# One replicated denominator operand per chunk instead of one per head

## The chip, the cores and the metric

The kernel runs on all 8 cores of one Trainium2 chip, each core on its own part of the tokens and with no exchange between cores. The metric is the device time of the slowest core, in microseconds (us). In the names of the profile PE is TensorE, DVE is VectorE, ACT is ScalarE, POOL is GpSimd and SP is SyncE.

## The reference

One transformer layer on x of shape (4, 4096, 1024): x + LN(attention(LN(x))), then x + LN(FFN(LN(x))). Attention is linear attention with 16 heads of width 64 and 64 features; the FFN is a block-diagonal "rail" expansion, a GELU and a product with a 1024 x 16384 matrix. What the change touches is the denominator of the attention:

```python
def step(carry, inp):
    kv_s, k_s = carry
    qc, kc, vc = inp
    kv_prod = jnp.einsum('bhtf,bhtd->bhtfd', kc, vc)
    kv_cum = jnp.cumsum(kv_prod, axis=2) + kv_s[:, :, None]
    k_cum = jnp.cumsum(kc, axis=2) + k_s[:, :, None]
    ctx = jnp.einsum('bhtf,bhtfd->bhtd', qc, kv_cum)
    den = jnp.maximum(jnp.einsum('bhtf,bhtf->bht', qc, k_cum), 1e-06)
    out_c = ctx / den[..., None]
    return ((kv_cum[:, :, -1], k_cum[:, :, -1]), out_c)
```

## The kernel before, in words

Two cores share a sequence of 4096 tokens. Each owns 2048 of them and goes over 2048 more ("carry") to get the state that stands ahead of its own; on the cores that own the first half this state is scaled by 0. Tokens lie on the free axis, in chunks of 256; channels lie on the partitions, in 8 blocks of 128.

Each chunk has two stages. Stage A (stageA_gen) normalises x, makes Q, K and V and the features of Q and K. Stage B (emit_stageB) does the attention of the chunk, head by head, then the output projection, the layer norm and the residual add L301 into x_sb. First come 8 carry chunks, stage A only, with the update of the state; then stage A of main chunk 0; then for each of 8 main chunks stage B, with stage A of the next chunk interleaved: ahead of each head, pump() lets the generator emit its next piece. There are 11 calls' worth of pieces, so the last heads of a chunk stand alone ("plain heads"), and all heads of the last chunk do. Last comes the FFN, in two halves of 1024 tokens, with its weights streamed in.

Nothing schedules the work: each engine runs its instructions in the order in which the Python code emits them. T_, V_ and A_ emit for TensorE, VectorE and ScalarE, and each such instruction raises its engine's semaphore (sem_pe, sem_dv, sem_ac). P.snap gives the count so far, and waits=[("dv", n)] makes an instruction wait until VectorE has raised its own to n. L83 is the line of this wait in the helper, so a wait for a semaphore of VectorE shows in the profile as "DVEq L83".

The state is held as S_f (fp32) and its bf16 image S_bf, which is columns 1856 to 2383 of the shared buffer railsM: 8 blocks of 66 columns, for heads 2b (partitions 0 to 63) and 2b+1 (partitions 64 to 127). Columns 0 to 63 of a block are the sum of k times v, column 64 is the sum of k. S_bf is refreshed once at the end of a chunk (L596); within a chunk only S_f moves.

One head hh (lo = 0 or 64, slot sl = hh % 2 in PSUM) runs so:

- VectorE, L509: column 64 of the head's block is copied 64 times side by side into denrep, a 64x64 operand (columns 1792 to 1855 of railsM). It waits for slot_dv[sl], the count of VectorE at the end of the head two before.
- TensorE, L516 and L523: scores of k against q, 256 and 128 columns, which wait for the same slot_dv[sl] and for the transposed k of the chunk.
- VectorE, L529: scores times the causal mask, into ab_bf (also in railsM).
- TensorE, eight matmuls L535 to L569 behind one wait for L529: context from the state and from the scores, denominator from the state (L549, whose stationary operand is denrep) and from the scores, and the state's increment.
- VectorE, L576: denominator, at least 1e-6; ScalarE, L580 and L583: its inverse through Ln and Exp; VectorE, L587: context times inverse; VectorE, L591: increment added to S_f. Then slot_dv[sl] is taken.

A piece of stage A, where one is pumped, stands ahead of L509 on VectorE and ahead of L516 on TensorE. Ahead of head 0 the piece is L381, a copy of x into bf16. SyncE and GpSimd issue no work in stage B.

Of the kernel before, what the change touches and what calls it, by code (L numbers as in the profile page):

```python
# [11 lines left out]
AP = bass.AP  # L12
# [81 lines left out]
def build_nc(debug=(), n_carry=NCH, n_main=NCH, do_ffn=True, dumps=()):  # L94
# [33 lines left out]
    with es:  # L128
        sb = lambda n, shp, dt: es.enter_context(nc.sbuf_tensor(n, list(shp), dt))
        x_sb = sb("x_sb", (128, DB * NOWN), F32)  # L130
        railsM = sb("railsM", (128, 32 * 128), BF16)
# [19 lines left out]
        P = Prog(list(sems))  # L151

        def T_(fn, waits=()):
            P.emit("tensor", fn, waits, "pe")

        def V_(fn, waits=()):
            P.emit("vector", fn, waits, "dv")
# [26 lines left out]
        for db in range(DB):  # L184
# [17 lines left out]
           waits=[("dv", d_sv)])  # L202
# [7 lines left out]
           waits=[("dv", d_sv2)])  # L210
# [4 lines left out]
           waits=[("ac", P.snap("ac"))])  # L215
# [26 lines left out]
        ab_bf = railsM[:, 3424:3808]  # L242
        S_f = sba("S_f", (128, 8 * 66), F32)
        S_bf = railsM[:, 1856:2384]
        denrep = railsM[:, 1792:1856]
        dinv = railsM[:, 1536:1792]
        f32sB = sba("f32sB", (128, 1024), F32)
        mrB = sba("mrB", (128, 512), BF16)
# [244 lines left out]
        def emit_stageB(ci, parity, pump):  # L493
            qfb, kfb, kTb, vab = qf2[parity], kf2[parity], kT2[parity], va2[parity]
            kfT_done = marks[ci]["kfT_done"]
            slot_dv = [P.snap("dv")] * 2
            for hh in range(H):
                pump()
                sl = hh % 2
                base = sl * 1024  # L500
                bb, lo = hh // 2, (hh % 2) * 64
                kwo = {} if sl == 0 else {"tile_position": (0, 64)}
                kws = {} if sl == 0 else {"tile_position": (64, 64)}
                kwa = {} if sl == 0 else {"tile_position": (64, 0)}
                ctx0 = base + 512
                den0 = base + 768
                dS0 = base + 384

                V_((lambda v, hh=hh, sl=sl, lo=lo: v.tensor_copy(  # L509
                    denrep[sl * 64:sl * 64 + 64, 0:64],  # L510
                    AP(railsM, lo * 4096 + 1856 + 66 * (hh // 2) + 64,
                       [[4096, 64], [0, 64]]))),
                   waits=[("dv", slot_dv[sl])])

                T_((lambda t, base=base, bb=bb, lo=lo, kwa=kwa, kfb=kfb, qfb=qfb:
                    t.matmul(  # L516
# [4 lines left out]
                   waits=[("dv", slot_dv[sl]), ("dv", kfT_done)])  # L521
# [23 lines left out]
                    psB[lo:lo + 64, ctx0 + 128:ctx0 + 256],  # L545
                    vab[:, 1056 + 66 * hh:1056 + 66 * hh + 64],
                    ab_bf[:, 256:384], start=False, stop=True, **kwo)))
                T_((lambda t, den0=den0, hh=hh, lo=lo, sl=sl, bb=bb, kws=kws,
                    qfb=qfb: t.matmul(  # L549
                        psB[lo:lo + 64, den0:den0 + 256],  # L550
                        denrep[sl * 64:sl * 64 + 64, 0:64],
                        qfb[lo:lo + 64, bb * 256:bb * 256 + 256],
                        start=True, stop=False, **kws)))
                T_((lambda t, den0=den0, lo=lo, kwo=kwo: t.matmul(
# [27 lines left out]
                   waits=[("dv", dd)])  # L582
# [17 lines left out]
            for ob in range(8):  # L600
                for db in range(DB):
# [5 lines left out]
                       waits=[("dv", scan_done)] if (ob == 0 and db == 0) else [])  # L607
            po = P.snap("pe")
            for ob in range(8):
# [4 lines left out]
                   waits=[("pe", po)] if ob == 0 else [])  # L614
# [338 lines left out]
```

How the kernel before makes its waits and increments, by code:

```python
            def body(engobj, ename, elist):  # L74
                deep = engobj is nc.vector or engobj is nc.scalar
                for idx, (waits, fn, inc, inc_n) in enumerate(elist):
                    for s, v in waits:
                        if v > 0:
                            engobj.wait_ge(prog.sems[s], v)
                    ins = fn(engobj)
                    if inc is not None and signal_for.get((ename, idx), False):
                        if deep:
                            engobj.drain(fusable=True).then_inc(
                                prog.sems[inc], inc_n)
                        else:
                            ins.then_inc(prog.sems[inc], inc_n)
```

## Time and profile before

| What | us |
|---|---|
| Median of 2 runs (lowest, highest) | 4408.71 (4405.87, 4411.55) |
| The profiled execution | 4407.01 |
| Its span, core 4 (the slowest) | 4405.5 |
| Span of its fastest core, core 0 | 4351.4 |
| First L509, core 4: stage B of chunk 0 begins | 814.3 |
| L690 clears railsM for the FFN, core 4 | 2357.4 |
| VectorE busy, 1894 instructions | 1084.3 |
| TensorE matmuls busy, 10368 instructions | 2250.1 |

The span runs from the first to the last instruction of a core. A timeline's first number is the start from there, the second the duration. A bracket behind an instruction tells how long its engine was idle before it, and what ended that: another engine's instruction, a semaphore wait (L83), or "issue", when the profile shows nothing that it waited for.

### The profile page before, as it was taken

Reading aid. Unit: us, or ns where it says so; the run is one execution under the profiler, and the core shown is the slowest. Engines: PE = TensorE matmul, PEld = TensorE weight load, DVE = VectorE, ACT = ScalarE, POOL = GpSimd, SP = SyncE. Lnnn points to the kernel's source line nnn. Section 1 sums busy time; section 2 is a strip of 40 time slices with the busy share of each in tenths; the row PEclk is TensorE's granted clock in tenths of the full one; section 3 lists DMA queues with packets and bytes.
Section 4 is the critical chain, followed back from the end, with each engine's and each line's share of the span. In section 5 each row is a group of like instructions: output and inputs, shape, how many; then the busy total and the mean of one; then the engine's idle time right before and its main releaser. Section 6 shows DMA issues by size and latency. Waiting matters only on the chain.

```text
span 4405.5 us, 30746 instructions; the slowest of 8 cores (4351.4 to 4405.5 us)
## 1 busy us (share of the span) xinstructions
PE 2250.1 (51%) x10368; PEld 1014.3 (23%) x10368; DVE 1084.3 (25%) x1894; ACT 774.1 (18%) x1065; POOL 51.4 (1%) x73
## 2 busy tenths in 40 slices
PE   1333434444444354444444566666665566666665
PEld 0222222222222222222222222222222222222222
DVE  0333333333333333333334200000003200000003
ACT  0211112211121212121210211111111211111111
POOL 1000000000000000000000000000000000000000
PEclk9666666666666666666655688888878688888887
DMA  7000000000000000000000222222223022222221
GB/s 161 5 10 5 5 10 0 0 1 1 1 0 1 0 1 0 0 1 1 1 1 6 39 39 38 38 39 38 38 38 67 10 38 38 39 38 39 38 39 38
DMA packets 55079, 99.57 MB, mean 23 GB/s; under 512 B 2368, under 2 KB 18880, under 8 KB 53824
## 3 DMA queue, kind: packets, MB, share of 16 engines
q0 software_dynamic: 44880, 80.82, 11.7%
q1 hardware_dynamic: 10048, 16.79, 1.2%
q8 instruction: 88, 1.44, 0.1%
q14 instruction: 63, 0.52, 0.0%
HBM read 170.03 MB, written 8.39 MB: 41 GB/s over the span
## 4 chain that ended last, share of the span: by engine, by line
PE 46%; DVE 23%; DMA 11%; ACT 10%; issue 7%; DVEq 2%; ACTq 0%; POOL 0%; SPq 0%; POOLq 0%
PE psB L804 23%; DMA wc<-wcT 8%; PE psA L396 5%; PE psA L767 3%; DVE oacc L822 3%; PE psA L429 3%; DVE qk_bf L406 2%; DVE railsM L529 2%; DMA xa_bf<-x_carry 2%; PE psB L602 2%; DVEq L83 1%; DVE f32s L319 1%; DVE pn_bf L346 1%; PE psA L272 1%; PE psA L339 1%
## 5 line engine op out<-in xcount | busy, mean ns | idle before, releaser
L804 PE MATMUL psB<-hsl,wc 128*128 128x512 bf16 x4096 | 1048.8, 402 | 557.9 <-DMA wc<-wcT 437.6
L804 PEld LDWEIGHTS psB<-hsl,wc 128*128 128x128 bf16 x4096 | 374.6, 101 | 1097.7 <-issue 771.7
L778 ACT ACTIVATE hsl<-psA 128x512 bf16<-128x512 f32 x512 | 305.7, 597 | 1347.7 <-PE psA L767 1345.4
L822 DVE TENSOR_TENSOR oacc<-oacc,psB 128x2048 f32<-128x2048 f32 x56 | 128.1, 2287 | 1440.7 <-PE psB L804 1440.7
L396 PE MATMUL psA<-ln_bf,wqkv_bf 128*128 128x256 bf16 x1536 | 248.9, 340 | 85.2 <-DVEq L83 85.2
L266 PE MATMUL psA<-xa_bf,allones_bf 128*128 128x256 bf16 x256 | 58.9, 409 | 377.3 <-DMA xa_bf<-x_carry 215.2
L767 PE MATMUL psA<-ln,railsM 32*128 32x512 bf16 x512 | 207.1, 407 | 22.7 <-DVEq L83 13.5
L396 PEld LDWEIGHTS psA<-ln_bf,wqkv_bf 128*128 128x128 bf16 x1536 | 182.8, 122 | 145.8 <-issue 90.8
L580 ACT ACTIVATE f32sB<-f32sB 64x256 f32<-64x256 f32 x128 | 53.0, 414 | 869.3 <-DVEq L83 869.3
L429 PE MATMUL psA<-wqkv_bf,ln_bf 128*128 128x512 bf16 x512 | 168.7, 503 | 34.2 <-DVEq L83 34.2
L339 PE MATMUL psA<-qk_bf,omega_bf 64*64 64x256 bf16 x384 | 50.9, 414 | 211.4 <-DVEq L83 211.4
L262 ACT ACTIVATE sq_bf<-xa_bf 128x2048 bf16<-128x2048 bf16 x32 | 61.1, 1909 | 552.6 <-DVEq L83 299.5
L535 PE MATMUL psB<-qf_a,railsM 64*64 64x256 bf16 x64 | 22.1, 345 | 259.5 <-DVEq L83 259.5
L535 PE MATMUL psB<-qf_b,railsM 64*64 64x256 bf16 x64 | 23.4, 366 | 245.1 <-DVEq L83 245.1
L406 DVE TENSOR_SCALAR qk_bf<-psA,bqkv_sb 128x256 bf16<-128x256 f32 x192 | 92.8, 483 | 202.0 <-PE psA L396 183.0
L314 PE MATMUL psA<-sq_bf,blockones_bf 128*128 128x256 bf16 x192 | 47.4, 398 | 152.8 <-ACTq L83 116.2
L266 PEld LDWEIGHTS psA<-xa_bf,allones_bf 128*128 128x128 bf16 x256 | 32.6, 136 | 396.9 <-issue 384.8
L576 DVE TENSOR_SCALAR f32sB<-psB 64x256 f32<-64x256 f32 x128 | 54.0, 422 | 241.9 <-PE psB L569 239.5
L767 PEld LDWEIGHTS psA<-ln,railsM 32*128 32x128 bf16 x512 | 46.7, 92 | 254.7 <-issue 254.7
L429 PEld LDWEIGHTS psA<-wqkv_bf,ln_bf 128*128 128x128 bf16 x512 | 60.4, 123 | 136.1 <-issue 113.1
L587 DVE TENSOR_TENSOR ctx_bf<-psB,railsM 64x256 bf16<-64x256 f32 x128 | 54.0, 422 | 151.7 <-ACTq L83 151.7
L319 DVE TENSOR_SCALAR f32s<-psA 128x1024 f32<-128x1024 f32 x48 | 58.8, 1225 | 113.5 <-PE psA L314 113.5
(150 smaller groups left out, 2064.0 us busy)
## 6 DMA issues: line engine op xcount, KB each, us to landing
wc<-wcT POOLq DMA_DIRECT2D x32, 2048.0 KB, 18.3
x_sb<-x_own SPq DMA_DIRECT2D x8, 1024.0 KB, 23.3
y_out<-oacc SPq DMA_DIRECT2D x8, 1024.0 KB, 4.4
wqkv_bf<-wqkvT POOLq DMA_DIRECT2D x8, 768.0 KB, 48.8
xa_bf<-x_carry POOLq DMA_DIRECT2D x8, 512.0 KB, 6.1
wout_bf<-woutT POOLq DMA_DIRECT2D x8, 256.0 KB, 67.8
rut_bf<-rut POOLq DMA_DIRECT2D x4, 128.0 KB, 6.1
omega_bf<-omega POOLq DMA_DIRECT2D x2, 128.0 KB, 16.0
```

What stands on the lines that cost most here:

```text
L266: T_((lambda t, db=db: t.matmul(ps[:, 0:256], allones_bf[:, :], xb[:, db * 256:(db + 1) * 256], start=(db == 0), stop=(db == DB - 1))), wa ...
L319: V_((lambda v: v.tensor_scalar(f32s[:, 0:1024], psA[:, 0:1024], 1e-24, None, op0=ALU.max)), waits=[("pe", p0)])
L339: t.matmul(psA[lo:lo + 64, bb4 * 256:(bb4 + 1) * 256], omega_bf[lo:lo + 64, hcur * 64:(hcur + 1) * 64], src_bf[lo:lo + 64, bb * 256:(bb + ...
L396: T_((lambda t, jj=jj, jb=jb, db=db: t.matmul(psA[:, jj * 256:(jj + 1) * 256], wqkv_bf[:, db * 3072 + jb * 128:db * 3072 + (jb + 1) * 128] ...
L406: v.tensor_scalar(dst[:, dstoff + jj * 256:dstoff + (jj + 1) * 256], psA[:, jj * 256:(jj + 1) * 256], bqkv_sb[:, jb0 + jj:jb0 + jj + 1], N ...
L429: T_((lambda t, sub=sub, db=db, oh=oh: t.matmul(psA[:, oh * 512:(oh + 1) * 512], ln1_bf[:, db * 256 + sub * 128:db * 256 + sub * 128 + 128 ...
L529: V_((lambda v, base=base: v.tensor_tensor(ab_bf[:, 0:384], psB[:, base:base + 384], mask384_bf[:, 0:384], op=ALU.mult)), waits=[("pe", pa)])
L602: T_((lambda t, ob=ob, db=db: t.matmul(psB[:, ob * 256:(ob + 1) * 256], wout_bf[:, db * 1024 + ob * 128:db * 1024 + (ob + 1) * 128], ctx_b ...
L767: zsl=zsl: t.matmul(psA[:, zsl * 512:(zsl + 1) * 512], railsM[rg * 32:(rg + 1) * 32, q4 * 128:(q4 + 1) * 128], ln3[pbase:pbase + 32, dbl * ...
L778: A_((lambda a, fcl=fcl, zsl=zsl, hb=hb: a.activation(hb[:, fcl * 512:(fcl + 1) * 512], psA[:, zsl * 512:(zsl + 1) * 512], AF.Gelu)), wait ...
L804: t.matmul(psB[:, ob * 512:(ob + 1) * 512], wcbufs[fcl // 8][:, (fcl % 8) * 1024 + obi * 128: (fcl % 8) * 1024 + (obi + 1) * 128], hb[:, f ...
L822: V_((lambda v, g=g, obg=obg: v.tensor_tensor(AP(oacc, obg * 4096 + g * 512, [[8 * 1024, 128], [1024, 4], [1, 512]]), AP(oacc, obg * 4096 ...
```

## The change

The per-head copy L509 is taken out. In its place one copy at the start of emit_stageB, ahead of head 0, replicates column 64 of all 8 blocks of S_bf, on all 128 partitions, into a new denrep of 512 columns (2384 to 2895 of railsM, free in this stage). It waits for all TensorE work emitted so far. slot_dv is taken behind it, so the first two heads' score matmuls wait for it too. The denominator matmul reads the 64 columns of its own block.

```diff
-        denrep = railsM[:, 1792:1856]
+        denrep = railsM[:, 2384:2896]
...
             kfT_done = marks[ci]["kfT_done"]
+            V_((lambda v: v.tensor_copy(
+                AP(railsM, 2384, [[4096, 128], [64, 8], [1, 64]]),
+                AP(railsM, 1856 + 64, [[4096, 128], [66, 8], [0, 64]]))),
+               waits=[("pe", P.snap("pe"))])
             slot_dv = [P.snap("dv")] * 2
...
-                V_((lambda v, hh=hh, sl=sl, lo=lo: v.tensor_copy(
-                    denrep[sl * 64:sl * 64 + 64, 0:64],
-                    AP(railsM, lo * 4096 + 1856 + 66 * (hh // 2) + 64,
-                       [[4096, 64], [0, 64]]))),
-                   waits=[("dv", slot_dv[sl])])
...
-                        denrep[sl * 64:sl * 64 + 64, 0:64],
+                        denrep[lo:lo + 64, bb * 64:bb * 64 + 64],
```

The order of the instructions on the other engines stays; on VectorE it changes at two kinds of places. VectorE before the change, at the start of main chunk 1 (L301 is the residual add of chunk 0, L278 to L285 the first steps of a layer norm of stage A):

```order
L301 TENSOR_TENSOR x_sb<-x_sb,ctx_bf 128x8x256
L381 CAST xa_bf<-x_sb 128x2048 [waits sem_din]
L509 COPY railsM<-railsM 64x64 [waits sem_dv]
L529 TENSOR_TENSOR railsM<-psB,railsM 128x384 [waits sem_pe]
L576 TENSOR_SCALAR f32sB<-psB 64x256 [waits sem_pe]
L587 TENSOR_TENSOR ctx_bf<-psB,railsM 64x256 [waits sem_ac]
L591 TENSOR_TENSOR S_f<-S_f,psB 64x65
L278 TENSOR_SCALAR f32s<-psA 128x256 [waits sem_pe]
L280 TENSOR_TENSOR f32s<-f32s 128x256
L282 SCALAR_TENSOR_TENSOR f32s<-psA,f32s 128x256
```

and VectorE at the same place after the change, where L496 is the new copy, and the lines from L527 on are those from L529 on of before, numbered two lower:

```order
L301 TENSOR_TENSOR x_sb<-x_sb,ctx_bf 128x8x256
L496 COPY railsM<-railsM 128x512 [waits sem_pe]
L381 CAST xa_bf<-x_sb 128x2048 [waits sem_din]
L527 TENSOR_TENSOR railsM<-psB,railsM 128x384 [waits sem_pe]
L574 TENSOR_SCALAR f32sB<-psB 64x256 [waits sem_pe]
L585 TENSOR_TENSOR ctx_bf<-psB,railsM 64x256 [waits sem_ac]
L589 TENSOR_TENSOR S_f<-S_f,psB 64x65
L278 TENSOR_SCALAR f32s<-psA 128x256 [waits sem_pe]
L280 TENSOR_TENSOR f32s<-f32s 128x256
L282 SCALAR_TENSOR_TENSOR f32s<-psA,f32s 128x256
```

The new copy stands between L301 and L381, with a wait for sem_pe, and the mask multiply follows L381 directly. VectorE in the last chunk's first two heads, before:

```order
L301 TENSOR_TENSOR x_sb<-x_sb,ctx_bf 128x8x256
L509 COPY railsM<-railsM 64x64 [waits sem_dv]
L529 TENSOR_TENSOR railsM<-psB,railsM 128x384 [waits sem_pe]
L576 TENSOR_SCALAR f32sB<-psB 64x256 [waits sem_pe]
L587 TENSOR_TENSOR ctx_bf<-psB,railsM 64x256 [waits sem_ac]
L591 TENSOR_TENSOR S_f<-S_f,psB 64x65
L509 COPY railsM<-railsM 64x64 [waits sem_dv]
L529 TENSOR_TENSOR railsM<-psB,railsM 128x384 [waits sem_pe]
```

and after:

```order
L301 TENSOR_TENSOR x_sb<-x_sb,ctx_bf 128x8x256
L496 COPY railsM<-railsM 128x512 [waits sem_pe]
L527 TENSOR_TENSOR railsM<-psB,railsM 128x384 [waits sem_pe]
L574 TENSOR_SCALAR f32sB<-psB 64x256 [waits sem_pe]
L585 TENSOR_TENSOR ctx_bf<-psB,railsM 64x256 [waits sem_ac]
L589 TENSOR_TENSOR S_f<-S_f,psB 64x65
L527 TENSOR_TENSOR railsM<-psB,railsM 128x384 [waits sem_pe]
```

From the second head on the mask multiply stands directly behind the add into S_f, where the copy stood between them; this is so in every head ahead of which no piece of stage A stands, and in the others it stands directly behind the piece.

## Rows read from the trace of the kernel before

**Rows 1.** The page's first line, all cores.

```profile
span 4405.5 us, 30746 instructions; the slowest of 8 cores (4351.4 to 4405.5 us)
```

**Rows 2.** The page's chain that ended last, shares of the span by engine.

```profile
PE 46%; DVE 23%; DMA 11%; ACT 10%; issue 7%; DVEq 2%; ACTq 0%; POOL 0%; SPq 0%; POOLq 0%
```

**Rows 3.** Who waited, core 4: engine, tile, line <- releaser: us, times, longest.

```profile
PE psB L535 <- DVEq L83: 504.5, 128, 9.1
```

**Rows 4.** VectorE's groups: line, operation, tiles, count | busy us, mean ns | idle before.

```profile
L529 DVE TENSOR_TENSOR railsM<-psB,railsM 128x384 bf16<-128x384 f32 x128 | 71.4, 558 | 25.4 <-issue 24.9 <-PE psB L523 0.5
...
L319 DVE TENSOR_SCALAR f32s<-psA 128x1024 f32<-128x1024 f32 x48 | 58.8, 1225 | 113.5 <-PE psA L314 113.5
...
L576 DVE TENSOR_SCALAR f32sB<-psB 64x256 f32<-64x256 f32 x128 | 54.0, 422 | 241.9 <-PE psB L569 239.5 <-PE psA L396 2.4
...
L509 DVE COPY railsM<-railsM 64x64 bf16<-64x64 bf16 x128 | 24.2, 189 | 26.4 <-DVEq L83 26.4
...
L328 DVE TENSOR_SCALAR xa_bf<-xa_bf 128x1024 bf16<-128x1024 bf16 x48 | 20.5, 426 | 118.4 <-ACTq L83 118.4
...
L596 DVE CAST railsM<-S_f 128x528 bf16<-128x528 f32 x8 | 3.5, 435 | 0.9
```

**Rows 5.** Timeline of one plain head: start, duration, engine, line [idle before <-releaser].

```profile
1981.79 0.21 DVE L591 TENSOR_TENSOR S_f<-S_f,psB 64x65 f32<-64x65 f32 x1
1982.19 0.19 DVE L509 COPY railsM<-railsM 64x64 bf16<-64x64 bf16 x1 [0.19 <-DVEq L83]
1982.57 0.56 DVE L529 TENSOR_TENSOR railsM<-psB,railsM 128x384 bf16<-128x384 f32 x1 [0.19 <-issue]
...
1983.31 0.39 PE L535 MATMUL psB<-qf_b,railsM 64*64 64x256 bf16 x1 [3.32 <-DVEq L83]
...
1985.18 0.43 DVE L576 TENSOR_SCALAR f32sB<-psB 64x256 f32<-64x256 f32 x1 [2.05 <-PE psB L569]
1985.19 0.31 PE L523 MATMUL psB<-qf_b,kf_b 64*128 64x128 bf16 x1
...
1988.11 0.56 DVE L529 TENSOR_TENSOR railsM<-psB,railsM 128x384 bf16<-128x384 f32 x1 [0.19 <-issue]
```

**Rows 6.** Timeline, VectorE, a copy behind L591.

```profile
1161.23 0.23 DVE L591 TENSOR_TENSOR S_f<-S_f,psB 64x65 f32<-64x65 f32 x1
1161.64 1.23 DVE L460 COPY kT_a<-psT 128x2048 bf16<-128x2048 bf16 x1 [0.19 <-issue]
```

**Rows 7.** Timeline, first heads of main chunk 1 and of the last chunk.

```profile
1223.09 1.23 DVE L381 CAST xa_bf<-x_sb 128x2048 bf16<-128x2048 f32 x1 [0.19 <-issue]
...
1223.36 0.31 PE L523 MATMUL psB<-qf_a,kf_a 64*128 64x128 bf16 x1
...
2240.56 0.19 DVE L509 COPY railsM<-railsM 64x64 bf16<-64x64 bf16 x1 [0.19 <-DVEq L83]
...
2241.24 0.56 DVE L529 TENSOR_TENSOR railsM<-psB,railsM 128x384 bf16<-128x384 f32 x1 [0.49 <-PE psB L523]
```

**Rows 8.** Stretches from L301 to L301: length, busy by engine, granted clock, DMA, GB/s.

```profile
1013.22:1220.61 207.39, 92.67 (x484) 52.81 (x484) 71.58 (x138) 39.20 (x52) 0.00 (x0) 0.62 0.00 0
...
1627.02:1828.98 201.96, 87.11 (x484) 50.75 (x484) 71.58 (x138) 39.20 (x52) 0.00 (x0) 0.63 0.00 0
...
2033.75:2238.08 204.33, 88.82 (x484) 51.44 (x484) 71.58 (x139) 39.20 (x52) 0.00 (x0) 0.63 0.00 1
2238.08:2354.02 115.94, 47.33 (x240) 25.39 (x240) 39.59 (x96) 15.99 (x35) 0.00 (x0) 0.56 0.00 0
```

**Rows 9.** Timeline, V's projection at both clocks; L576 behind a head at the high clock.

```profile
1954.53 5.60 PE L429 MATMUL psA<-wqkv_bf,ln_bf 128*128 128x512 bf16 x16
...
1964.34 3.63 PE L429 MATMUL psA<-wqkv_bf,ln_bf 128*128 128x512 bf16 x16
...
1057.29 0.43 DVE L576 TENSOR_SCALAR f32sB<-psB 64x256 f32<-64x256 f32 x1 [1.41 <-PE psB L569]
```

**Rows 10.** Who waited, core 4, in the FFN.

```profile
PE psB L804 <- DMA wc<-wcT: 437.6, 14, 33.2
```

More of the change, by code:

```diff
@@ L547, in emit_stageB @@
                     ab_bf[:, 256:384], start=False, stop=True, **kwo)))
-                T_((lambda t, den0=den0, hh=hh, lo=lo, sl=sl, bb=bb, kws=kws,
+                T_((lambda t, den0=den0, hh=hh, lo=lo, bb=bb, kws=kws,
                     qfb=qfb: t.matmul(
                         psB[lo:lo + 64, den0:den0 + 256],
-                        denrep[sl * 64:sl * 64 + 64, 0:64],
+                        denrep[lo:lo + 64, bb * 64:bb * 64 + 64],
                         qfb[lo:lo + 64, bb * 256:bb * 256 + 256],
```

## The prediction

> **What bounds the kernel now.** I read the cores first: they end between 4351.4 and 4405.5 us [rows 1]; the last is core 4, and every number below is its own. The profiled execution took 4407.0 us for a span of 4405.5, so 1.5 us lie outside the span; the median of the runs shown is 4408.7, 1.7 above it, and I add nothing for that. The chain that ended last names no single engine: TensorE 46%, VectorE 23%, DMA 11%, ScalarE 10% [rows 2]. That is the picture of stages that take turns. The change touches one of them, the part of attention that I call stage B. There the question is whether VectorE's small copy L509 is in the chain or beside it; its 0.55% share of the span says nothing of that.
>
> Two readings settle it. First, who waits in stage B: TensorE stands before L535 in all 128 heads, 504.5 us in total, for VectorE [rows 3]. L535 is released by the mask multiply L529. So TensorE is the one that waits, and whatever stands ahead of L529 on VectorE delays it. Second, what ended the wait of L529 itself: 24.9 of its 25.4 us of idle time are "issue", and 0.5 us are TensorE's L523, in one head only [rows 4]. So the two score matmuls L516 and L523, which write what L529 reads, are finished in 127 of 128 heads before VectorE gets there. One plain head shows it: S_f's add L591 ends at 1982.00, the copy runs 1982.19 to 1982.38, the mask starts at 1982.57, and TensorE, idle for 3.32 us, starts L535 at 1983.31; the next head's L523 runs from 1985.19 to 1985.50, while that head's mask comes only at 1988.11, 2.6 us later [rows 5]. The copy and the gap that belongs to it are in series with everything in a head. That holds in heads with a piece of stage A too, since the piece's VectorE work comes before the copy and its TensorE work before L516.
>
> **What goes.** In each of 127 heads the stretch from the end of L591 (or of a piece of stage A) to the start of L529 is gap, copy, gap. By group: 24.2 us of copies and 26.4 us of idle time before them, over 128: 0.189 + 0.206 = 0.395 us a head [rows 4]. The 0.19 before L529 stays, if the mask standing directly behind L591 starts as soon after it as after a copy. Rows show this: L460, a copy that waits for a TensorE semaphore long raised, as L529 will, stands directly behind L591 and starts 0.19 us after its end [rows 6]. So 127 x 0.395 = 50.2 us go. In the 128th, head 0 of the last chunk, the copy is hidden: VectorE had 0.49 us more to wait for L523 anyway [rows 7]. It gives nothing. L549, which reads the replicated column, reads as many columns and partitions as before and stays as it is.
>
> **What comes.** Eight copies of 128x512, one a chunk, behind L301 and ahead of head 0. The trace has no such copy. Nearest by shape is L509 itself with its repeated element: 64 columns in 0.189 us. Nearest by size is L596, 528 columns in 0.435 us, fp32 to bf16 [rows 4]. From the two, (0.435 - 0.189) / 464 = 0.53 ns a column: 512 columns are 0.43 us, which I take. Below it cannot be faster than L509's 0.19; above, at the rate of operations that read PSUM, (1.225 - 0.558) / (1024 - 384) = 1.04 ns a column from L319 and L529, it takes 0.558 + 128 x 1.04 ns = 0.69 us. With a gap of 0.19 that is 0.62 us a chunk, 5.0 us in all (3.0 to 7.1).
>
> L328, a bf16 operation, moves 1024 columns in 0.426 us [rows 4], which would suggest 0.29 us for 512. The Trainium skill says why this does not carry over (Vector Engine (DVE) Microarchitecture Reference, section 5.1): pairing two 16-bit values in a read wants an innermost step of 1, and a one-source copy that repeats an element takes the mode that splits the work over two ports instead, two results a cycle. By that rule the copy costs 0.43 us; by L328's it would cost 0.29, a difference of 1 us over eight.
>
> Is all of it on the path? slot_dv is now taken behind the copy, so L516 and L523 of head 0 wait for it, and they start 0.62 us later. In seven chunks L381 (1.23 us) follows the copy on VectorE, covers both matmuls, which were done at 1223.67, 0.65 us before it was [rows 7], so that their own delay costs nothing. The copy itself is in VectorE's queue and delays L381 and the mask by its whole 0.62 us. In the last chunk there is no L381: L516, L523 and then the mask follow the copy in series, again 0.62 us. So 8 x 0.62 in full. Its TensorE semaphore is no wait: all TensorE work emitted before it is the layer norm whose sums L278 has consumed, or in chunk 0 the transposes behind L460. Nothing is queued behind it that a DMA needs; SyncE and GpSimd have no work in stage B.
>
> **The sum.** 50.2 - 5.0 = 45.2 us, all before the FFN, which starts that much earlier on all eight cores together. 4407.0 - 45.2 = **4361.8 us**, 1.0% less. I write 4362.
>
> **What the clock and the FFN add to the range.** TensorE's granted clock in stage B is a mixture of 1.2 and 2.4 GHz: 0.62 to 0.63 of full in chunks with stage A, 0.56 in the last [rows 8]. The same instructions took 207.39 us in one chunk and 201.96 in another; the mean of six is (2238.08 - 1013.22) / 6 = 204.14 [rows 8]. Shorter heads shift where the clock rises and falls. If all seven chunks fell like the best one, 7 x 2.2 = 15 us more would go; all like the worst, 7 x 3.3 = 23 us would come back. In the FFN TensorE waits 437.6 us for weights [rows 10] and the cores differ by 54 us at the end [rows 1], though their order hardly changes when all shift alike; I allow 5 us. With the copy's ends (2 us either way) the likeliest case runs from 4362 - 22 = 4340 to 4362 + 30 = 4392.
>
> **Rivals.**
>
> *Only the copy's own time goes.* If the 0.206 us ahead of the copy is the tail of L591 (its drain and signal) and the mask would have to sit through it besides its own, each head gives 0.189: 127 x 0.189 - 5.0 = 19 us, so 4388. For it: the gap before L509 is of the same size as other gaps. Against: [rows 6]. Chance 7%.
>
> *The clock rises with the denser heads.* A head at the low clock waits 2.05 us for L569, one at the high clock 1.41, and 239.5 us over 127 waits is a mean of 1.89, so about a quarter of the heads run at the high clock: (2.05 - 1.89) / 0.64 [rows 4, 5, 9]. If the other 95 turned, 95 x 0.64 = 61 us more would go, and pieces like V's projection would fall from 5.60 to 3.63 us [rows 9]; of the 56 pieces of that size in seven chunks I take a quarter as cold now, 14 x 1.97 = 28 us more. 4362 - 61 - 28 = 4273, past the 2% that about marks what a measurement here can tell from no change. For it: L535's idle stretch falls from 3.32 to 2.94 us. The Trainium skill (TensorE: Matmul & The Clock Gate, What's actually happening) has the clock throttled by default and released by activity, which points this way. Against: the last chunk, whose heads are all plain, holds 0.56 [rows 8] though TensorE's long idle stretch is 3.3 of each 5.54 us there, and 0.4 of 5.54 us is a small change. Chance 6%; a partial form of it is in the lower part of the range.
>
> *The clock falls out of step (slower).* The dense pieces of stage A and the output projection are worth most of the high-clock time. Going cold costs 5.60 - 3.63 = 1.97 us for 16 x 512 columns [rows 9]. A chunk has 4 x 32 x 256 + 2 x 16 x 512 + 64 x 256 = 65,536 columns of such work, eight times that: at most 15.8 us a chunk, 110 us in seven. All cold would give 4362 + 110 = 4472, slower than before. It decides against the change from a loss of 45.2 / 7 = 6.5 us a chunk, some three of eight such pieces. Against it: the worst chunk so far lies 3.3 above the mean, and TensorE becomes busier, not idler. Chance 4%.
>
> *Forecast*: 83%.
>
> **Chances.** Forecast 83 (all within 2%, which is 88 us), copy's time only 7 (within 2%), clock up 6 (faster by over 2% in 5 of them), clock down 4 (mostly within 2%, over it in 2). Faster by over 2%: 0.05; within: 0.93; slower: 0.02. The range is the likeliest case's own, 4340 to 4392, which takes in the copy-only case at 4388 and leaves out the two cases of the clock, one in ten.
>
> **What would show each step.** Right: no copy between L591 and the mask, 0.19 us between them, plain heads 0.38 to 0.40 us shorter (5.54 to 5.14); eight copies of about 0.43 us; six middle chunks with a mean near 198.4 us (204.14 - 16 x 0.395 + 0.62); TensorE's wait before L535 down by about 50 us; the FFN from 2354 on unchanged in length within some 10 us. Wrong: the mask waiting on L523 in many heads, a gap of 0.4 us behind L591, a copy over 0.7 us, a granted clock in stage B that differs by more than 0.02, or an FFN that grows by as much as stage B loses.

## The result and the profile after

The ratio of the changed kernel to the one before is 0.9899, 95% interval 0.9871 to 0.9927: about 45 us less, between 32 and 57. The median of 15 runs is 4368.4 us, that of 14 runs of the kernel before 4413.2; the ratio leaves out the runs in which the cores of one die were granted a lower clock than the others. The forecast was 4362 us, 1.0% less, with 93% on a change within 2%. The profiled execution of the changed kernel took 4352.8 us, its slowest core is core 3.

VectorE's groups of the changed kernel, core 3, with the columns of [rows 4]:

```profile
L527 DVE TENSOR_TENSOR railsM<-psB,railsM 128x384 bf16<-128x384 f32 x128 | 71.3, 557 | 25.5 <-issue 24.6 <-PE psB L521 0.9
L574 DVE TENSOR_SCALAR f32sB<-psB 64x256 f32<-64x256 f32 x128 | 54.0, 422 | 242.9 <-PE psB L567 242.9
L496 DVE COPY railsM<-railsM 128x512 bf16<-128x512 bf16 x8 | 3.4, 427 | 1.5 <-issue 1.5
```

The new copy takes 0.427 us, eight times, with a gap of 0.19 (1.5 / 8) and no wait for TensorE. The mask L527 still waits for nothing but the hand-over from the instruction ahead of it (0.19 us), save one head with 0.9 us. TensorE's wait ahead of the first matmul behind the mask fell from 504.5 us [rows 3] to this, in the view of who waited:

```profile
PE psB L533 <- DVEq L83: 459.3, 128, 8.7
```

That is 45.2 us less, on the engine that waits, where about 50 were forecast (the two profiles' slowest cores are compared; core for core it is 43 to 46). Most of what is missing is in the seven heads behind the 16 transposes L454 on TensorE. On core 4 these took 1.8 to 1.9 us in all seven chunks before, at the low clock, and some 1.1 us in five of the seven after, at the high one; TensorE was ready earlier there and waited longer. The timeline of the last chunk's first heads, the same place as the lower rows of [rows 7]:

```profile
2205.03 2.29 DVE L301 TENSOR_TENSOR x_sb<-x_sb,ctx_bf 128x2048 f32<-128x2048 f32 x1
2207.51 0.43 DVE L496 COPY railsM<-railsM 128x512 bf16<-128x512 bf16 x1 [0.19 <-issue]
2208.80 0.56 DVE L527 TENSOR_TENSOR railsM<-psB,railsM 128x384 bf16<-128x384 f32 x1 [0.86 <-PE psB L521]
...
2213.54 0.22 DVE L589 TENSOR_TENSOR S_f<-S_f,psB 64x65 f32<-64x65 f32 x1
2213.94 0.56 DVE L527 TENSOR_TENSOR railsM<-psB,railsM 128x384 bf16<-128x384 f32 x1 [0.19 <-issue]
...
2218.69 0.23 DVE L589 TENSOR_TENSOR S_f<-S_f,psB 64x65 f32<-64x65 f32 x1
2219.10 0.56 DVE L527 TENSOR_TENSOR railsM<-psB,railsM 128x384 bf16<-128x384 f32 x1 [0.19 <-issue]
```

Two things are to be seen. Between L589 and the mask 0.18 to 0.19 us are left, and a plain head takes 5.16 us (2213.94 to 2219.10) where it took 5.54. And in head 0 the mask starts 3.77 us behind L301's start, where it started 3.16 behind it (2241.24 against 2238.08 [rows 7, 8]): the copy with its gap, 0.61 us, is in the chain there, and nothing is gained.

**Where the time went, stage by stage.** From the first instruction of stage B of chunk 0 (L516 before, the new copy after) to the last start of L301, the mean over the eight cores is 1539.9 us before and 1502.0 after, 37.9 less, where 45.2 were forecast. VectorE works or waits through all of it, so its time can be split without a rest. In us from the start of the first mask on, mean over eight cores; "own" is its work (537.0 before, 515.9 after) with the gaps that no other engine ended (96.7 and 72.4):

| Kernel | VectorE's own | waits for TensorE | waits for ScalarE | together |
|---|---|---|---|---|
| before | 633.7 | 602.7 | 301.7 | 1538.2 |
| after | 588.3 | 609.9 | 301.8 | 1500.0 |

VectorE's own time fell by 45.4 us, which is what the prediction's sum gave. The 7 us that are missing are in its waits for TensorE, and TensorE's instructions are the same. What changed is the clock that they were granted. In that stretch V's projections L429 kept TensorE busy for 73.2 us where it was 67.6 (mean of the six cores whose profile has all their records), the output projection 72.6 for 69.0, the projections of Q and K 145.5 for 149.9, and the transposes 9.1 for 12.9. These last 3.8 us give VectorE nothing, since it does not wait for the transposes. VectorE's wait for one of V's two buffers, core 4 before and core 3 after:

```profile
L443 DVE CAST va_b<-psA 128x1024 bf16<-128x1024 f32 x8 | 9.8, 1224 | 22.0 <-PE psA L437 22.0
L443 DVE CAST va_b<-psA 128x1024 bf16<-128x1024 f32 x8 | 9.8, 1225 | 27.5 <-PE psA L437 27.5
```

A plain head became 0.38 us shorter and not 0.395. Most gaps ahead of L509 are 0.187 us; the mean of 0.206 holds seven longer ones, as this in VectorE's timeline of the kernel before:

```profile
2302.57 0.19 DVE L509 COPY railsM<-railsM 64x64 bf16<-64x64 bf16 x1 [0.54 <-DVEq L83]
```

Such gaps are not the copy's. VectorE has 11 of them in stage B before, ahead of L509, L529 and L610, and 5 after, at the same instructions on all eight cores, and they follow each other at distances near multiples of 48 of its instructions. But with six fewer of them another 2.1 us went, so that the mean was a fair price after all: 127 x 0.38 + 2.1 - 5.0 = 45.4. Without them the sum is 43.3 us. The chunks, L301 to L301, with the columns of [rows 8] (core 3):

```profile
1010.32:1204.94 194.62, 84.69 (x484) 49.26 (x484) 68.99 (x123) 39.20 (x52) 0.00 (x0) 0.64 0.00 0
1204.94:1404.64 199.70, 88.96 (x484) 51.03 (x484) 68.98 (x123) 39.20 (x52) 0.00 (x0) 0.62 0.00 0
1404.64:1605.97 201.33, 92.21 (x484) 52.39 (x484) 68.97 (x123) 39.20 (x52) 0.00 (x0) 0.60 0.00 0
...
2205.03:2316.47 111.44, 48.48 (x240) 25.83 (x240) 36.98 (x81) 16.00 (x35) 0.00 (x0) 0.55 0.00 0
2316.47:4351.30 2034.83, 1300.01 (x4992) 468.57 (x4992) 295.93 (x322) 354.72 (x564) 31.33 (x37) 0.79 0.21 38
```

The same 484 matmuls keep TensorE busy for 84.69 us in one chunk and for 92.21 in another, VectorE's 68.98 and ScalarE's 39.20 us stay, and the chunk is 6.7 us longer: what varies is the clock that TensorE is granted. The last row is the FFN, 2034.8 us on the slowest core, against 2051.5 on the slowest before (2354.05 to 4405.50); over all cores the mean is 2016.8 against 2025.7. The FFN's share of the difference between the two profiled executions is no effect of the change, as the repeats below show.

### The profile page after: what moved, and what is told of

It is laid out like the page before. It is cut to its first block, busy times and chain, and to the rows that moved or that the text cites. A ratio compares the mean times of both kernels' runs of the same rounds, so it can differ in the third digit from the quotient of the medians.

```text
span 4351.3 us, 30386 instructions; the slowest of 8 cores (4319.0 to 4351.3 us)
## 1 busy us (share of the span) xinstructions
PE 2271.1 (52%) x10368; PEld 1014.9 (23%) x10368; DVE 1063.5 (24%) x1774; ACT 774.2 (18%) x1065; POOL 51.4 (1%) x73
## 4 chain that ended last, share of the span: by engine, by line
PE 47%; DVE 23%; DMA 11%; ACT 10%; issue 7%; DVEq 2%; ACTq 0%; POOL 0%; SPq 0%; POOLq 0%
PE psB L802 24%; DMA wc<-wcT 8%; PE psA L396 5%; PE psA L765 3%; DVE oacc L820 3%; PE psA L429 3%; DVE qk_bf L406 2%; PE psB L600 2%; DVE railsM L527 2%; DMA xa_bf<-x_carry 2%; DVE pn_bf L346 1%; DVE f32s L319 1%; PE psA L272 1%; DVEq L83 1%; PE psA L339 1%
## 5 line engine op out<-in xcount | busy, mean ns | idle before, releaser
L802 PE MATMUL psB<-hsl,wc 128*128 128x512 bf16 x4096 | 1062.2, 406 | 525.7 <-DMA wc<-wcT 405.4
L429 PE MATMUL psA<-wqkv_bf,ln_bf 128*128 128x512 bf16 x512 | 177.9, 524 | 33.5 <-DVEq L83 33.5
L339 PE MATMUL psA<-qk_bf,omega_bf 64*64 64x256 bf16 x384 | 50.9, 413 | 211.4 <-DVEq L83 211.4
L406 DVE TENSOR_SCALAR qk_bf<-psA,bqkv_sb 128x256 bf16<-128x256 f32 x192 | 92.8, 483 | 196.3 <-PE psA L396 177.3
L429 PEld LDWEIGHTS psA<-wqkv_bf,ln_bf 128*128 128x128 bf16 x512 | 62.5, 127 | 142.5 <-issue 124.6
L323 ACT ACTIVATE f32s<-f32s 128x1024 f32<-128x1024 f32 x48 | 50.7, 1056 | 203.1 <-DVEq L83 203.1
(150 smaller groups left out, 2051.5 us busy)
## 6 DMA issues: line engine op xcount, KB each, us to landing
wqkv_bf<-wqkvT POOLq DMA_DIRECT2D x8, 768.0 KB, 48.6
```

The costliest lines, as they stand in the source:

```text
L339: t.matmul(psA[lo:lo + 64, bb4 * 256:(bb4 + 1) * 256], omega_bf[lo:lo + 64, hcur * 64:(hcur + 1) * 64], src_bf[lo:lo + 64, bb * 256:(bb + ...
L406: v.tensor_scalar(dst[:, dstoff + jj * 256:dstoff + (jj + 1) * 256], psA[:, jj * 256:(jj + 1) * 256], bqkv_sb[:, jb0 + jj:jb0 + jj + 1], N ...
L429: T_((lambda t, sub=sub, db=db, oh=oh: t.matmul(psA[:, oh * 512:(oh + 1) * 512], ln1_bf[:, db * 256 + sub * 128:db * 256 + sub * 128 + 128 ...
L802: t.matmul(psB[:, ob * 512:(ob + 1) * 512], wcbufs[fcl // 8][:, (fcl % 8) * 1024 + obi * 128: (fcl % 8) * 1024 + (obi + 1) * 128], hb[:, f ...
```

## The experiments

"Stage B" in this section is the stretch just named, from its first instruction to the last start of L301, mean over eight cores. "By the rows" is what the instructions on VectorE account for against 1539.9 us before: 0.38 us for a small copy that leaves the chain of a head, 0.62 us for a chunk's copy. These sums leave out the longer gaps, whose number changes from kernel to kernel (11 before, 5 after) and with it up to 2.4 us; the table behind the last profiles has them in.

### One copy more per head

```diff
+                # the same L509 again, directly behind itself
+                V_(... v.tensor_copy(denrep[sl * 64:sl * 64 + 64, 0:64], ...),
+                   waits=[("dv", slot_dv[sl])])
```

> The kernel before with L509 issued twice in each head. Theory (each such copy is in the chain of 127 heads): every head grows by 0.395 us, plain heads from 5.54 to 5.93 us, the whole by 50 us, ratio 1.011. Rival (VectorE has slack, the copy is mostly hidden and the change's gain came from the clock or the FFN): under 15 us, ratio below 1.004. On the clock: if the length of a chunk depends on where the clock's changes fall, the six middle chunks will not all be 6.3 us longer but scatter by some 5 us around that.

Measured: ratio 1.0138, interval 1.0052 to 1.0223. VectorE's groups of this kernel:

```profile
L509 DVE COPY railsM<-railsM 64x64 bf16<-64x64 bf16 x128 | 24.2, 189 | 24.8 <-DVEq L83 24.8
L514 DVE COPY railsM<-railsM 64x64 bf16<-64x64 bf16 x128 | 24.2, 189 | 24.8 <-DVEq L83 24.8
```

A second copy costs 0.189 + 0.194 us in every head, 48.6 us in 127 heads, as the theory says; the rival with a hidden copy falls, since the interval excludes it. Stage B is 1598.7 us, 58.8 more, so 10 us come on top: VectorE's waits for TensorE are 612.5 us for 602.7. The six chunks did not scatter here: on all cores all are between 211.4 and 211.8 us. That part of the expectation was wrong.

### The same copies behind the mask

```diff
-                V_(... tensor_copy(denrep ...), waits=[("dv", slot_dv[sl])])
...
                 da = P.snap("dv")
+                V_(... tensor_copy(denrep ...))
+                dc = P.snap("dv")
...
-                        start=True, stop=False, **kws)))
+                        start=True, stop=False, **kws)), waits=[("dv", dc)])
```

> The kernel before with all 128 small copies kept, but each issued behind its head's mask multiply, and L549 waiting for it. Theory (it is the place on VectorE and not the work): the copy runs while VectorE would wait 2.05 us for TensorE, it ends 0.3 to 0.4 us behind the mask, L549 comes 0.9 us or more behind it and does not wait; heads as short as after the change (5.15 us), 50 us less than before, ratio about 0.9885, with VectorE's busy time unchanged at 1084 us. Rival (the 20 us less of VectorE's work is what counts, or the shorter program): no more than 10 us gained.

Measured: ratio 0.9888, interval 0.983 to 0.9947, stage B 1492.5 us, where the rows give 1539.9 - 48.3 = 1491.6. The timeline of a plain head:

```profile
2239.74 0.56 DVE L523 TENSOR_TENSOR railsM<-psB,railsM 128x384 bf16<-128x384 f32 x1 [0.19 <-issue]
2240.41 0.19 DVE L527 COPY railsM<-railsM 64x64 bf16<-64x64 bf16 x1
2240.47 0.39 PE L535 MATMUL psB<-qf_b,railsM 64*64 64x256 bf16 x1 [2.97 <-DVEq L83]
...
2241.25 0.42 PE L549 MATMUL psB<-qf_b,railsM 64*64 64x256 bf16 x1
2241.60 0.42 PE L554 MATMUL psB<-railsM,allones_bf 128*64 128x256 bf16 x1
...
2242.34 0.42 DVE L576 TENSOR_SCALAR f32sB<-psB 64x256 f32<-64x256 f32 x1 [1.75 <-PE psB L569]
...
2244.88 0.56 DVE L523 TENSOR_TENSOR railsM<-psB,railsM 128x384 bf16<-128x384 f32 x1 [0.19 <-issue]
```

The copy ends at 2240.60, L549 starts at 2241.25 in its turn, and the copy only takes 0.3 us out of VectorE's wait for L569 (1.75 for 2.05). The head is 5.14 us long. All 128 copies are still there (VectorE's busy time is 1084.9 us), and the time is that of the changed kernel: what the change gained was their place ahead of the mask, not their work. This is shown, and the rival of less work falls. (The copies have no wait for a semaphore here; the next experiment has the price of that, 0.07 us each.)

### The small copy without its wait

```diff
-                   waits=[("dv", slot_dv[sl])])
+                   )
```

> The kernel before, with the small copy L509 left in its place but without its wait for VectorE's own semaphore. Theory (the copy and a gap of 0.206 us that belongs to its wait are in series with the head): the idle time ahead of the copy falls from 0.206 to about 0.12 us, the gap that L591 has behind L587 without a wait; 0.09 us a head, 11 us in all, ratio to before about 0.9975, and plain heads of 5.45 us for 5.54. Rival (the gap is the tail of L591, its drain and signal, and no wait's doing): the gap stays at 0.2 us and the time stays.

Measured: ratio 0.9988, interval 0.9952 to 1.0025, which cannot tell 0.9975 from 1. The group can:

```profile
L509 DVE COPY railsM<-railsM 64x64 bf16<-64x64 bf16 x128 | 24.2, 189 | 15.4 <-issue 0.4
```

The mean gap fell from 26.4 / 128 = 0.206 to 0.120 us, the usual one from 0.187 to 0.118. So 0.07 us of each gap were the wait for VectorE's own semaphore, which had long been raised, and 0.12 belong to one more instruction in the queue; the other 0.017 of the mean are longer gaps, of which seven stood ahead of the copy before and one here. The theory holds for the gap: 9 us for the waits, 10 with the longer gaps. VectorE's own time fell by 9.5 us. Stage B is 1535.7 us, only 4.2 less: 5.4 us came back in VectorE's waits for TensorE.

### The chunk's copy where VectorE waits for the output projection

```diff
-            V_(chunk copy, waits=[("pe", P.snap("pe"))])
+            if ci == 0:
+                V_(chunk copy, waits=[("pe", P.snap("pe"))])
...
             V_((lambda v: v.tensor_copy(S_bf[:, :], S_f[:, :])))
             scan_done = P.snap("dv")
+            if ci + 1 < n_main:
+                V_(chunk copy, waits=[("pe", pc)])
```

> The changed kernel with the chunk's copy for chunks 1 to 7 issued directly behind the refresh of S_bf (L594) of the chunk before, where VectorE waits 9 us for the output projection. Theory: 7 x 0.62 = 4.3 us less than after the change, ratio to before about 0.9889 against 0.9899; the last chunk's mask of head 0 starts 3.16 us behind L301's start instead of 3.77. Rival (the copy at the chunk's start is hidden already beside TensorE's first scores): the same start of the mask and no gain. The total cannot tell these apart within its interval, the timeline can.

Measured: ratio 0.9913, interval 0.9878 to 0.9949, no better than the change itself. Core 0's timeline, the last chunk:

```profile
2189.43 0.43 DVE L595 CAST railsM<-S_f 128x528 bf16<-128x528 f32 x1
2190.05 0.43 DVE L598 COPY railsM<-railsM 128x512 bf16<-128x512 bf16 x1 [0.19 <-issue]
...
2213.31 2.29 DVE L301 TENSOR_TENSOR x_sb<-x_sb,ctx_bf 128x2048 f32<-128x2048 f32 x1
2216.47 0.56 DVE L528 TENSOR_TENSOR railsM<-psB,railsM 128x384 bf16<-128x384 f32 x1 [0.86 <-PE psB L522]
```

The mask starts 3.16 us behind L301 again, as forecast, so the 0.61 us a chunk did leave the chain. Yet stage B is 1503.6 us, 11 above what the rows give (1539.9 - 43.3 - 4.3 = 1492.3): the 4 us were won and lost again. VectorE's waits for TensorE, which should be 4 us shorter with the copy in them, are 611.6 us for 609.9, and V's projections took 78.0 us for 73.2.

### The changed kernel again, and with a shift in time

> The changed kernel itself, once more, for its chunk lengths alone (from L301 to L301). If these are set by the program and the point at which the clock's changes fall in it, they should lie between 194 and 203 us again with a mean of 198 to 200 over six chunks and eight cores, but need not have the same order as in the first profile.

> The changed kernel with one extra write of a scratch buffer on VectorE at the start of stage B of chunk 0 only, some 1.1 us, so that all that follows is later against the clock's changes and else the same. Theory (what a chunk gives back or gains through TensorE's clock depends on when the clock changes fall in it, and not on the shorter heads as such): the chunks' lengths take other values than in the other runs of the changed kernel, in the same band of 194 to 203 us, and their mean stays within 1.5 us. Rival (the give-back of 0.7 us a chunk is a property of heads of 5.15 us): the same mean to 0.2 us and the same list.

```diff
             slot_dv = [P.snap("dv")] * 2
+            if ci == 0:
+                V_(lambda v: v.memset(f32sB[:, 0:1024], 0.0))
```

Measured: 4372.4 us for the repeat and 4364.5 for the shift, one execution each. The repeat's chunks have a mean of 198.5 us (the first profile's 198.9), and its first two are 196.3 and 198.0 on all eight cores, as on five cores of the first profile. The shift (the write took 0.91 us) gives other ones, core 0:

```profile
1006.52:1206.98 200.46, 90.14 (x483) 51.64 (x484) 68.97 (x123) 39.20 (x52) 0.00 (x0) 0.64 0.00 0
1206.98:1405.65 198.67, 88.00 (x483) 50.71 (x484) 68.99 (x123) 39.20 (x52) 0.00 (x0) 0.63 0.00 0
1405.65:1600.26 194.61, 84.38 (x483) 49.26 (x484) 68.99 (x123) 39.20 (x52) 0.00 (x0) 0.64 0.00 0
```

with a mean of 198.7 over all. Core 0 had 196.33, 198.00 and 199.65 us there in the first profile, so single chunks move by up to 5 us when the program is 1 us later. They can do so without a shift too: core 4 had 200.62 and 202.01 us in its first two chunks in the first profile and 196.33 and 198.00 in the repeat. The mean moves by less than 0.5 either way, so these two runs don't tell a shift's mean from a repeat's. Stage B is 1498.9 us in the repeat and 1500.6 in the shifted kernel (1501.7 less the write and its gap, which lie in it there), against 1502.0; the slowest core's FFN was 2053.0 and 2048.3 us, against 2034.8 in the first profile and 2051.5 before. The 17 us by which the first profile's FFN was shorter on the slowest core were luck of that execution.

Where the clock takes time is best seen in a piece with no other engine in it, the 64 matmuls of the output projection. Timelines of the first profile of the changed kernel, core 3:

```profile
1379.76 10.02 PE L600 MATMUL psB<-ctx_bf,wout_bf 128*128 128x256 bf16 x64 [3.23 <-DVEq L83]
...
1781.78 8.72 PE L600 MATMUL psB<-ctx_bf,wout_bf 128*128 128x256 bf16 x64 [3.25 <-DVEq L83]
```

Both start after the same idle time and the same heads. The stretches of the two, with the granted clock behind the engines' columns:

```profile
1379.76:1389.78 10.02, 10.02 (x64) 7.51 (x64) 0.00 (x0) 0.00 (x0) 0.00 (x0) 0.70 0.01 2
1781.78:1790.50 8.72, 8.72 (x64) 6.91 (x64) 0.00 (x0) 0.00 (x0) 0.00 (x0) 0.81 0.00 0
```

A mean of 0.70 of 2.4 GHz against 0.81: the granted clock rose from 1.2 to 2.4 GHz at 1385.68 in the one, 5.9 us behind its start, and at 1785.04 in the other, 3.3 behind it.

### The kernel before again, and with the same shift

The rows give 1496.6 us for stage B of the changed kernel, and its profiles show more. Either the first profile of the kernel before was a lucky draw of the clock, or the clock answers to the change.

> The kernel before, once more, for its chunks. Theory (its first profile was a favourable draw of the clock): the mean of the six middle chunks rises from 203.9 us to 204.3 or more, and stage B from 1539.9 us to 1542 to 1550, so that the changed kernels fall into line with what the rows give. Rival (it is no draw: the clock answers in its own way to the length of a head): again 203.9 within 0.3, and stage B again within 2 us of 1539.9. The plain head is 5.54 us by both, and the time 4400 to 4425 us.

> The kernel before with one write of about 0.9 us ahead of the first head, the shift given to the changed kernel before. Theory (a favourable draw): other single chunks, and with them a mean of the six middle chunks at 204.3 us or more and stage B at 1542 to 1550 us. Rival: single chunks move, the mean stays at 203.9 within 0.3 us and stage B within 3 us of 1540.

```diff
             slot_dv = [P.snap("dv")] * 2
+            if ci == 0:
+                V_(lambda v: v.memset(f32sB[:, 0:1024], 0.0))
```

Measured, in the profiled executions: 4457.7 us (4514.8 in another one) and 4398.9. The first time can't be compared, since it is made in the FFN: cores 0 and 1 took 2095.6 and 2093.1 us for it at a granted clock of 0.76, the others 2001 to 2055 at 0.80. In stage B two other cores stand apart, 2 and 3, which were granted 0.58 to 0.59 in chunk 0 and the first three middle chunks where 0.62 to 0.63 stand on the rest. With them the mean of the chunks is 204.3 us and stage B 1543.4; the six other cores have 203.9 and 1539.6. Core 0's first two chunks in that profile, where it had 204.27 and 201.86 before:

```profile
1023.15:1227.44 204.29, 89.36 (x483) 51.88 (x484) 71.59 (x139) 39.20 (x52) 0.00 (x0) 0.63 0.00 0
1227.44:1429.29 201.85, 86.66 (x483) 50.63 (x484) 71.59 (x138) 39.20 (x52) 0.00 (x0) 0.63 0.00 0
```

And core 0 with the shift:

```profile
1014.44:1219.20 204.76, 89.72 (x483) 51.89 (x484) 71.61 (x139) 39.20 (x52) 0.00 (x0) 0.62 0.00 0
1219.20:1420.10 200.90, 86.01 (x483) 50.18 (x484) 71.58 (x139) 39.20 (x52) 0.00 (x0) 0.64 0.00 0
```

With the shift the mean is 202.7 us and stage B 1535.1, less the write and its gap. So the theory of a lucky draw falls: in the repeat four of the six cores drew chunks of the first profile again, and another moment gives less time, not more. The rival is right for the repeat and wrong for the shift, whose mean moved by 1.3 us (202.4 to 203.0 on its cores, 203.1 to 204.2 on those without the shift); it is one profile. Like for like, stage B is 39 us shorter by the change without the shift (1539.8 against 1500.5, the means of two profiles each) and 35 with it (1535.1 against 1500.6). The split of VectorE's time, as in the result's table (the repeat of the kernel before without cores 2 and 3):

| Kernel | VectorE's own | waits for TensorE | waits for ScalarE | together |
|---|---|---|---|---|
| before | 633.7 | 602.7 | 301.7 | 1538.2 |
| before, again | 633.9 | 602.2 | 301.7 | 1537.9 |
| before, shifted | 632.9 | 599.6 | 300.9 | 1533.3 |
| changed | 588.3 | 609.9 | 301.8 | 1500.0 |
| changed, again | 588.5 | 606.5 | 301.8 | 1496.8 |
| changed, shifted | 588.3 | 608.9 | 301.1 | 1498.4 |
| one copy more per head | 682.8 | 612.5 | 301.3 | 1596.6 |
| small copy without its wait | 624.2 | 608.1 | 301.6 | 1534.0 |
| small copies behind the mask | 624.2 | 565.3 | 301.6 | 1491.1 |
| chunk's copy late | 588.3 | 611.6 | 301.7 | 1501.5 |

VectorE's own time is the same in every profile of one kernel to 0.2 us. By the change it falls by 45.4 us without the shift and by 44.6 with it. TensorE gave back 6 us without the shift and 9 with it.

### The masks one head ahead

The experiments say that any instruction of VectorE between a head's context multiply and the next mask is in series with TensorE. The mask itself, and the way through ScalarE, need not be. In this version the scores of head h+1 are issued directly behind the matmuls of head h, its mask between the maximum and the context multiply of head h, and the next piece of stage A behind head h's work instead of ahead of head h+1's scores. Head 0's piece, scores and mask come ahead of the loop:

```diff
-                pump()
...
+                if hh + 1 < H:
+                    pa = scores(hh + 1)      # the two score matmuls
                 V_(... f32sB ... 1e-6, op0=ALU.max ...), waits=[("pe", pc)])
                 dd = P.snap("dv")
+                if hh + 1 < H:
+                    da = mask(hh + 1, pa)    # the mask multiply
                 A_(... AF.Ln ...)
                 A_(... AF.Exp ...)
                 V_(... ctx_bf ...)
                 V_(... S_f ...)
                 slot_dv[sl] = P.snap("dv")
+                if hh + 1 < H:
+                    pump()
```

> The changed kernel with each head's mask multiply moved further forward on VectorE: the mask of head h+1 is issued right behind the maximum of head h (L574 there), where VectorE waits 1.18 us for ScalarE, and the scores of head h+1 directly behind head h's matmuls, with the next piece of stage A behind them. Theory (what VectorE does between a head's context multiply and the next mask is in series with TensorE, and so is the way through ScalarE): a plain head is then mask 0.56, matmuls 2.05, maximum 0.42 and a gap of 0.19, 3.2 us instead of 5.15; 15 x 1.9 = 29 us in the last chunk, and about 30 us in each of seven pumped chunks (5 plain heads of 1.9, ten heads with a piece of 2 or so), together 240 us, to about 4130, ratio to before 0.936 (range 0.92 to 0.96). Rival (the chain is bound elsewhere, by pieces of stage A through ScalarE and VectorE): only the plain heads gain, 29 + 7 x 9.5 = 95 us, ratio 0.968.

> The run with the masks ahead, and the chunk's copy behind the refresh of S_bf as well. Theory: 4 us less than that run, at most; within the intervals no difference. It is run as the version that could be the fastest, on the same chip as the other.

Measured: ratio 0.9297 (0.9255 to 0.9339) and 0.9285 (0.9238 to 0.9332), medians 4109.5 and 4100.0 us. The two cannot be told apart. VectorE's timeline of the first, a plain head:

```profile
1965.03 0.42 DVE L586 TENSOR_SCALAR f32sB<-psB 64x256 f32<-64x256 f32 x1 [0.84 <-PE psB L577]
1965.63 0.56 DVE L523 TENSOR_TENSOR railsM<-psB,railsM 128x384 bf16<-128x384 f32 x1 [0.19 <-issue]
1966.63 0.42 DVE L599 TENSOR_TENSOR ctx_bf<-psB,railsM 64x256 bf16<-64x256 f32 x1 [0.44 <-ACTq L83]
1967.16 0.21 DVE L603 TENSOR_TENSOR S_f<-S_f,psB 64x65 f32<-64x65 f32 x1
1968.24 0.43 DVE L586 TENSOR_SCALAR f32sB<-psB 64x256 f32<-64x256 f32 x1 [0.86 <-PE psB L577]
1968.86 0.56 DVE L523 TENSOR_TENSOR railsM<-psB,railsM 128x384 bf16<-128x384 f32 x1 [0.19 <-issue]
```

The head is 3.23 us long, the 3.2 of the expectation, and the mask now fills VectorE's wait for ScalarE (0.44 us left of 1.18). TensorE's wait ahead of the first matmul behind the mask:

```profile
PE psB L543 <- DVEq L83: 104.5, 79, 2.7
```

It was 459.3 us in 128 heads. The last chunk fell from 111.4 to 81.8 us, 29.6 where 29 were expected, and the middle chunks from 198.9 to 161.2 on average, 37.8 where 30 were expected. Five plain heads make 1.93 x 5 = 9.7 of that; the other 28 come from eleven heads with a piece of stage A, 2.6 us each. The rival, in which only plain heads gain, falls. The granted clock of these chunks rose too, to a mean of 0.67 from 0.63. Three things moved at once here (scores, mask, pieces), and no run parts them.

## Why the prediction was right, point by point

- **The copy is in the chain, in 127 of 128 heads.** Right, and shown from both sides: one more copy a head makes the kernel longer by about as much as the change made it shorter, and the same copies behind the mask cost nothing.
- **0.395 us a head, 50.2 us.** Right, with a little luck. A plain head became 0.38 us shorter, and 127 x 0.38 are 48.3. The mean gap that the prediction took also held seven longer gaps that belong to no copy; six fewer of these in the changed kernel gave the other 2 us. Between L589 and the mask stand 0.18 to 0.19 us. The rival "only the copy's own time goes" (4388 us) falls by that gap. It was in the range, and the total's interval reaches close to it (0.9927 is 4381 us); the rows decide it, not the total.
- **Eight copies of 0.43 us and 0.19 us of gap, all on the path, 5.0 us.** Right: 0.427 and 0.19, and the mask of the last chunk's head 0 came 0.61 us later. Two results a cycle for a repeated element (the Trainium skill, Vector Engine (DVE) Microarchitecture Reference, section 5.1) had given the prediction an estimate of 0.43 us, and the trace agrees with its 0.427.
- **45.2 us in all, TensorE's wait down by about 50.** VectorE's own time fell by 45.4 us, stage B by 37.9; the ratio gives 45 with 12 either way. That the total came out so near the forecast is in part luck, since stage B gave 7 us less. TensorE's wait fell by 45.2 us and not by 50, the most of that behind the transposes that ran at the high clock.
- **The clock's edge of 15 us gained to 23 us lost.** The size was right and the middle was not: the prediction took it as even. Against the first profile of before, VectorE's waits for TensorE were 7, 4 and 6 us longer in the three profiles of the changed kernel (its repeat and the shift among them), 5 without the wait and 10 with two copies; with the late copy 13 us came back and with the copies behind the mask 2 to 3. That the profile of before was a lucky draw was tried and fell. So a small part of what VectorE gives up comes back as TensorE's time at the lower clock, 6 to 9 us of 45 for this change, like for like. In the total this hardly shows, since the FFN of single executions varies by more.
- **The FFN unchanged within some 10 us.** The first profile missed this by 7 us (17 shorter); with three profiles of the changed kernel, at 2034.8, 2053.0 and 2048.3 us on the slowest core against 2051.5, no effect of the change is seen, and single profiles of one program differ by 18 us there, more than the 10 us of that line.
- **The rivals of the clock.** Neither came in the size that was named. The granted clock of middle chunks stayed at a mean of 0.63. What did come is a small form of the second: at the same mean clock the high stretches fell in other places, V's projections and the output projection took 9 us more, those of Q and K 4 less, and the transposes 4 less, for which VectorE does not wait. The rise did come, to 0.67, when a head fell to 3.2 us.

What stays open: how the clock's part follows from the length of a head. It is no simple rule of "shorter heads, slower clock", since the kernel with two copies, with longer heads, lost too, and the one with the copies behind the mask lost only 2 to 3 us with a head of 5.14 us. It depends on the moment, and perhaps differently in the two kernels (a shift of 0.91 us moved the mean chunk by 1.3 us in one and by less than 0.5 in the other, one profile each). No run varied the length of a head finely enough.

## What to carry to other kernels

An instruction's share of the span does not tell its price. Ask instead what ended the wait of the instruction behind it: here the mask waited for nothing but its place in VectorE's queue, and each copy of 0.19 us ahead of it cost 0.38 with its gap, 127 times. If what an operand needs is known early, issue it where the engine waits in any case. And when one small instruction turns out to be in the chain, look at all that share its place: moving scores, mask and pieces, so that the mask fills the wait for ScalarE, was worth six times the copy.

## What the hardware showed that was not expected

A wait for a semaphore that is long raised is not free: 0.07 us on VectorE (the usual gap 0.187 with it, 0.118 without), about a third of such a small copy. VectorE has longer gaps of some 0.5 us that belong to no instruction but to its place: 11 in stage B before, the same on all eight cores and in the repeat, at distances near multiples of 48 of its instructions, and 8 in other places when one write was added ahead. The same 64 matmuls behind the same idle time took 8.72 or 10.02 us, by when TensorE's clock rose from 1.2 to 2.4 GHz, and in this program, whose stages repeat with one period, these draws are not independent. The kernel before drew the same chunks in a second profile on four of six cores, within 0.02 us on core 0's first two, and a start 0.91 us later drew others. With two copies a head, 48 chunks on eight cores all lay within 0.4 us, all of them some 1.5 us above what the rows give (211.6 against 203.9 + 16 x 0.383 = 210.1).
